# Three of four chunks of the experts' second layer by parts, one high part cast on GpSimd

## The chip, the cores and the metric

The kernel runs on one core of a Trainium2 chip. The metric is the time on the device in microseconds (us) of one launch, from the first instruction to the last with what lies around them. Seven things work side by side on the core and meet only through semaphores: TensorE (PE; its weight loads are listed as PEld), VectorE (DVE), ScalarE (ACT), GpSimd (POOL), SyncE (SP), and the DMA engines.

## What is computed

Two transformer layers with residuals: an attention with inverse squared distances, a mixture of 8 experts with top-2 routing, a linear attention, and a block with top-k tokens. The change is in the second, whose part of the reference is:

```python
logits = jnp.einsum('bsd,de->bse', input_emb, Wr) + br
route_w = jax.nn.softmax(logits, axis=-1)
_, topk_idx = jax.lax.top_k(route_w, TOP_K)          # 2 of 8
mask = jax.nn.one_hot(topk_idx, E, dtype=route_w.dtype).sum(-2)
routed = route_w * mask
routed = routed / routed.sum(axis=-1, keepdims=True)
h = jax.nn.relu(jnp.einsum('bsd,edh->ebsh', input_emb, W1) + b1[:, None, None, :])
expert_out = jnp.einsum('ebsh,ehd->ebsd', h, W2) + b2[:, None, None, :]
return jnp.einsum('bse,ebsd->bsd', routed, expert_out)
```

There are 8 sequences of 512 tokens, 128 features, 8 experts with 512 hidden features each. All experts are computed for all tokens, and routing weights are zero for the others. All is float32.

## The kernel before, in words

The program has two parts: the attention, up to about 900 us of the trace, and the rest (`build_rest`), which is the part that matters here.

**The stream of chunks.** The experts' work is a stream of 256 chunks `n`: block `b = n // 32` is a sequence, `k = n % 32` a place in it, `g = n // 4` the pair of sequence and expert, `i = n % 4` the quarter of the 512 hidden features. Of each chunk TensorE makes `z` (first layer, 128 hidden features by 512 tokens, `hidden(n)`), ScalarE makes `hr = relu(z + b1)` from it, and TensorE adds its share of the second layer to `y` (`expert(n)`). At step `k` of block `b` TensorE does small things of other stages, then `expert(n)`, then `hidden(n + 6)`: z runs 6 chunks ahead. `z` and `y` have two PSUM banks each, so `hidden(n)` waits for the relu of chunk n-2.

**By parts.** A float32 matmul is one `nc.tensor.matmul` that the profile shows as two instructions. The other way, `product` (L74), splits each operand in a high part (rounded to the type float32r) and a low part (the rest), and adds three matmuls: high by high, low by high, high by low. The first layer is always by parts. The second layer is by parts for the chunks that `in_parts(n)` names: from the second block on (`n >= 32`), the odd ones, two of four. For these ScalarE evicts z twice (`hr_h` at L1011, `hr` at L1013) and GpSimd subtracts (`hr_l = hr - hr_h`, L963), in order of n. The parts of the weights, `w2s`, are made once by VectorE (`split_w2`, L1438 and L1440), at steps 24 to 31 of the first block. GpSimd does nothing else in this stage.

**The other stages.** Beside the stream run, for the next sequence f = b+1, the front chain (layernorm, router, softmax, ranks, routing weights) and, for the sequence t = b-1, the tail chain (linear attention, top-k block). Which step each piece stands at is written out by hand in a `step(b, k)` for each engine. Three places matter:

- VectorE at steps 22 to 26: `hand_over` splits the next sequence's input (L1343 a cast, L1345 a subtraction), `softmax_start` ends with L1315, for which ScalarE waits with its exponential (L977) before its relus of step 23; then the tail's division (L1378 to L1387), `softmax_end`, `expert_ranks` and `routing`, which ends with `rw` (L1338).
- TensorE at step 24, ahead of `expert(n)`: `turn_routing` (L1096) transposes `rw`, and waits for it.
- VectorE at steps 29 to 31: statistics, normalized tokens (L743), their scores (L1398, L1399); TensorE at step 29 transposes the scores (L1154), and waits for them.

TensorE's order is fixed, so what it waits for holds back all that stands behind.

Of the kernel before, what the change touches and what calls it, by code (L numbers as in the profile page):

```python
# [14 lines left out]
ALU = mybir.AluOpType  # L15
# [740 lines left out]
def build_rest(nc, ctx, a, ident, front, x1, rwd, out, first):  # L756
# [10 lines left out]
    with ExitStack() as own:  # L767
        def sb(name, shape, dt=F32):
            return own.enter_context(nc.sbuf_tensor(name, shape, dt))

        def psum(name, shape):
            return own.enter_context(nc.psum_tensor(name, shape, F32))


        w1 = sb("w1", [P, NE, FF])
        w2 = sb("w2", [P, NE * NF, D])
# [45 lines left out]

        scr = w1[:, :, :].rearrange("p (i c) t -> p i c t", i=2)
        above = sb("above", [P, 2, NC])
        keep = sb("keep", [P, 2, NC])

        w2s = [sb("w2_h", [P, NE * NF // 2, D], F32R), sb("w2_l", [P, NE * NF // 2, D], F32R)]
        hrs = [sb("hr_h", [P, HR // 2, T], F32R), sb("hr_l", [P, HR // 2, T], F32R)]
        eps_dec = sb("eps_dec", [P, NC])
# [6 lines left out]

        names = """w2s lo chain_l eps_dec in_x in_b2 in_rest_x in_last_x in_front in_tail ones2 w1s chain_f chain_t
                 stats_f mv_f std_f rstd_f xn_f turn_f xT_f logits exp rw rwT_ps rwT rwd rb xs z hr y ye ya yT_ps
# [19 lines left out]
        N_F = 13  # L858
        N_T, N_R = 11, 4

# [15 lines left out]
        def score_row(t):  # L876
            return z[:, 0, :] if t == LATE else tb[:, 1, :]
# [14 lines left out]
        def in_parts(n):  # L892
            return n >= NU and n % 2 == 1

# [57 lines left out]
        @block.gpsimd  # L952
        def _(pool):
            normalize = att_gpsimd(pool)
            normalize(NQ - 3)
            normalize(NQ - 2)
            normalize(NQ - 1)
            pool.wait_ge(att["x1_out"], 16 * B)
            nc.gpsimd.memset(kv[:, :, 2 * D:2 * D + 1], 1.0).then_inc(S["ones2"], 1)
            for n in range(NU + 1, B * NU, 2):  # L960
                m = n // 2
                pool.wait_ge(S["hr"], n + 1)
                nc.gpsimd.tensor_tensor(hrs[1][:, m % (HR // 2), :], hr[:, n % HR, :],  # L963
                                        hrs[0][:, m % (HR // 2), :].bitcast(F32), ALU.subtract).then_inc(S["lo"], 1)

        @block.scalar
        def _(act):
# [38 lines left out]
            def hidden(n):  # L1006
                act.wait_ge(S["z"], n + 1)
                if in_parts(n):
                    if n == NU + 1:
                        act.wait_ge(att["x1_out"], 16 * B)  # L1010
                    nc.scalar.activation(hrs[0][:, n // 2 % (HR // 2), :], z[:, n % 2, :], ACT.Relu,  # L1011
                                         bias=b1[:, n % NU:n % NU + 1])
                nc.scalar.activation(hr[:, n % HR, :], z[:, n % 2, :], ACT.Relu, bias=b1[:, n % NU:n % NU + 1]).then_inc(S["hr"], 1)  # L1013
# [59 lines left out]
        def _(pe):  # L1073
# [101 lines left out]
            def expert(n):  # L1175
# [5 lines left out]
                if n == NF:  # L1181
                    pe.wait_ge(S["rwT"], 1)
                if n == NU + 1:
                    pe.wait_ge(S["w2s"], NE * NF)
                pe.wait_ge(S["hr"], n + 1)
                if in_parts(n):
                    pe.wait_ge(S["lo"], (n - NU) // 2 + 1)
                    m = product(nc, y[:, g % 2, :], [w[:, k // 2, :] for w in w2s],
                                [v[:, n // 2 % (HR // 2), :] for v in hrs], start=False, stop=(i == NF - 1))
                else:  # L1190
                    m = nc.tensor.matmul(y[:, g % 2, :], w2[:, k, :], hr[:, n % HR, :], start=(i == 0), stop=(i == NF - 1))  # L1191
# [87 lines left out]
        def _(dve):  # L1279
# [121 lines left out]
            def token_ranks(t, c):  # L1401

                dve.wait_ge(S["score_ps"], t + 1)
                V.tensor_scalar(scr[:, 0, c, :], score_row(t), score[:, c:c + 1], None, ALU.is_gt, ALU.add, accum_out=above[:, 0, c:c + 1])
                ins = V.scalar_tensor_tensor(scr[:, 1, c, :], score_row(t), score[:, c:c + 1],
                                             ttri[:, (NC - 1 - c) * P:(2 * NC - 1 - c) * P], ALU.is_equal, ALU.mult,
                                             accum_out=above[:, 1, c:c + 1])
                if c == NC - 1:
                    lr(t, ins)

# [24 lines left out]
            def split_w2(e):  # L1435
                chunks = slice(NF // 2 * e, NF // 2 * (e + 1))
                source = w2[:, NF * e + 1:NF * (e + 1):2, :]
                V.tensor_copy(w2s[0][:, chunks, :], source).then_inc(S["w2s"], NF // 2)  # L1438
                dve.wait_ge(S["w2s"], NF * e + NF // 2)
                V.tensor_tensor(w2s[1][:, chunks, :], source, w2s[0][:, chunks, :].bitcast(F32),  # L1440
                                ALU.subtract).then_inc(S["w2s"], NF // 2)

# [18 lines left out]
            def step(b, k):  # L1461
# [77 lines left out]
                if (b, k) == (0, 21):  # L1539
                    add_output(B - 1)  # L1540
                if b == 0 and k >= 24:
                    if k == 24:
                        dve.wait_ge(att["x1_out"], 16 * B)
                    dve.wait_ge(in_w2[k - 24], 16)
                    split_w2(k - 24)

# [78 lines left out]
```

## Time and profile before

| | us |
|---|---|
| median of 3 runs | 1420.71 |
| lowest, highest | 1420.41, 1423.08 |
| the profiled execution, its own time | 1424.09 |
| its span, first to last instruction | 1422.3 |

Busy in the span: TensorE 1386.1 us (97%), ScalarE 1099.9 (77%), VectorE 1096.4 (77%), GpSimd 835.2 (59%). The experts' stream runs from about 920 to 1385 us, of which the seven blocks with chunks by parts take from 990 to 1385; behind it stands a tail of some 38 us for the last sequence.

In rows of the timeline the first number is the start from the span's start, the second the duration, both us; then engine, line, operation, output <- inputs, shapes and the number of merged instructions, and in brackets how long the engine had been idle and what ended that. L12 is line 12 of the kernel before.

### The profile page before, as it was taken

What the parts mean: (1) busy time and instruction counts of PE and PEld (TensorE: products, weight loads), DVE (VectorE), ACT (ScalarE), POOL (GpSimd) and SP (SyncE); (2) the same over time, 40 slices, a digit from 0 to 9 for tenths busy, and PEclk for the clock granted to TensorE, in tenths of its full rate; (3) what the DMA queues carried; (4) which work ended last, traced back from release to release, by engine and by line L of the source; (5) the groups of instructions that cost most, each with busy time, mean ns of one, the idle gap of its engine ahead of it and who ended that gap; (6) DMA issues with size and microseconds to landing.
All of it is one profiled execution on the core that took longest, in us unless ns stands there. A gap on an engine that the chain in (4) does not pass through costs nothing.

```text
span 1422.3 us, 18183 instructions
## 1 busy us (share of the span) xinstructions
PE 1386.1 (97%) x6496; PEld 744.1 (52%) x6496; DVE 1096.4 (77%) x1995; ACT 1099.9 (77%) x947; POOL 835.2 (59%) x655
## 2 busy tenths in 40 slices
PE   8999999999999999999999999899999999999995
PEld 5444444444444444444444444445777777777774
DVE  7887897788888887887888788635677686786757
ACT  2799889969978978979979979945676776776751
POOL 4568777778778778768867876411333333333330
PEclk9999999999999999999999999999999999999999
DMA  3000010011101101101101012343011010110100
GB/s 113 1 17 17 24 46 17 23 27 36 24 16 46 24 16 39 30 17 31 38 16 32 17 30 68 108 142 106 1 68 60 8 68 2 67 60 9 68 1 15
DMA packets 45705, 54.99 MB, mean 39 GB/s; under 512 B 13808, under 2 KB 32368, under 8 KB 44464
## 3 DMA queue, kind: packets, MB, share of 16 engines
q1 hardware_dynamic: 45616, 53.84, 12.7%
q8 instruction: 52, 0.85, 0.3%
q14 instruction: 37, 0.30, 0.1%
HBM read 48.97 MB, written 4.85 MB: 38 GB/s over the span
## 4 chain that ended last, share of the span: by engine, by line
PE 86%; DVE 8%; ACT 5%; issue 1%; DMA 0%; DVEq 0%; SPq 0%
PE sc L406 14%; PE av L419 13%; PE z L74 12%; PE pj L74 12%; PE y L1191 8%; PE sc L401 6%; PE y L74 5%; PE pj L383 4%; PE pj L451 4%; DVE w L597 3%; PE pj L429 2%; ACT w L684 1%; ACT w L688 1%; ACT w L680 1%; DVE high L565 1%
## 5 line engine op out<-in xcount | busy, mean ns | idle before, releaser
L597 DVE TENSOR_SCALAR w<-sc 128x1024 f32<-128x1024 f32 x256 | 301.2, 1217 | 69.4 <-PE sc L406 67.3
L680 ACT ACTIVATE w<-w 128x2048 f32<-128x2048 f32 x128 | 237.6, 1904 | 123.3 <-DVE w L597 123.0
L320 POOL TENSOR_TENSOR wsum<-wsum,w 128x512 f32<-128x512 f32 x248 | 317.6, 1281 | 19.4
L963 POOL TENSOR_TENSOR hr_l<-hr,hr_h 128x512 fp32r<-128x512 f32 x112 | 149.9, 1338 | 263.0 <-ACT hr L1013 263.0
L406 PE MATMUL sc<-query,key 64*128 64x512 f32 x1024 | 243.3, 594 | 0.0
L684 ACT ACTIVATE w<-w 128x2048 f32<-128x2048 f32 x128 | 240.1, 1899 | 0.4
L688 ACT ACTIVATE w<-w 128x2048 f32<-128x2048 f32 x128 | 239.8, 1897 | 0.0
L419 PE MATMUL av<-w,vt 128*64 128x512 f32 x1024 | 233.8, 598 | 2.6 <-ACT w L688 2.5
L1013 ACT ACTIVATE hr<-z,b 128x512 f32<-128x512 f32 x256 | 173.6, 685 | 67.8 <-PE z L74 67.7
L306 POOL TENSOR_TENSOR sqq<-query 128x512 f32<-128x512 f32 x63 | 65.5, 1040 | 187.1 <-DVE query L537 153.0
L317 POOL TENSOR_TENSOR wsum<-w 128x512 f32<-128x512 f32 x124 | 158.9, 1282 | 5.2 <-ACT w L688 5.2
L74 PE MATMUL z<-xs_h,w_h 128*128 128x512 f32 x256 | 158.0, 617 | 2.4 <-ACT hr L1013 2.1
L419 PEld LDWEIGHTS av<-w,vt 128*64 128x64 f32 x1024 | 67.8, 136 | 160.1 <-issue 138.8
L1191 PE MATMUL y<-hr,w 128*128 128x512 f32 x288 | 147.5, 593 | 0.0
L406 PEld LDWEIGHTS sc<-query,key 64*128 64x128 f32 x1024 | 97.7, 187 | 73.5 <-issue 62.5
L1011 ACT ACTIVATE hr_h<-z,b 128x512 fp32r<-128x512 f32 x112 | 76.7, 685 | 69.4 <-PE z L74 68.9
L326 POOL TENSOR_TENSOR hT<-hT,gT 128x1024 f32<-128x1024 f32 x32 | 76.4, 2389 | 52.4 <-DMA hT<-head_recips 52.4
L74 PE MATMUL z<-xs_l,w_h 128*128 128x512 f32 x256 | 100.9, 394 | 0.0
L604 DVE TENSOR_TENSOR gT<-av,gT 128x512 f32<-128x512 f32 x64 | 43.9, 686 | 73.8 <-PE av L419 73.8
L401 PE MATMUL sc<-qrow,krow 64*128 64x512 f32 x512 | 94.5, 446 | 6.4 <-DVE krow L586 5.6
L74 PE MATMUL z<-xs_h,w_l 128*128 128x512 f32 x256 | 100.4, 392 | 0.0
L401 PEld LDWEIGHTS sc<-qrow,krow 64*128 64x128 f32 x512 | 38.5, 185 | 105.7 <-issue 41.0
(213 smaller groups left out, 2360.5 us busy)
## 6 DMA issues: line engine op xcount, KB each, us to landing
hT<-head_recips SPq DMA_DIRECT2D x64, 256.0 KB, 4.0
rb<-routing SPq DMA_DIRECT2D x8, 2048.0 KB, 7.1
w<-in_W SPq DMA_DIRECT2D x16, 256.0 KB, 5.1
xa<-in_X SPq DMA_DIRECT2D x8, 256.0 KB, 4.5
xc<-in_X SPq DMA_DIRECT2D x8, 256.0 KB, 2.8
x<-xc SPq DMA_DIRECT2D x8, 256.0 KB, 4.0
x<-x SPq DMA_DIRECT2D x1, 1792.0 KB, 8.1
out<-prod SPq DMA_DIRECT2D x7, 256.0 KB, 2.3
```

The source lines that it names most:

```text
L74: m = nc.tensor.matmul(out, lhsT[u], rhs[v], start=start and i == 0, stop=stop and i == 2)
L317: nc.gpsimd.tensor_tensor(wsum[:, u, :], w[:, j % 2, u, 0, :], w[:, j % 2, u, 1, :], ALU.add).then_inc(s_added, 1)
L320: nc.gpsimd.tensor_tensor(wsum[:, u, :], wsum[:, u, :], w[:, j % 2, u, c, :], ALU.add).then_inc(s_added, 1)
L401: nc.tensor.matmul(sc[:, i, v, :], krow[halves[v], j % 2, g % 2, c * P:(c + 1) * P], qrow[halves[v], j % 2, :], start=True, stop=False)
L406: m = nc.tensor.matmul(sc[:, i, v, :], key[halves[v], g % 3, c * P:(c + 1) * P], query[halves[v], g % 3, :], start=False, stop=True)
L419: m = nc.tensor.matmul(av[64 * v:64 * v + 64, :], vt[:, c, (2 * g + v) * E0:(2 * g + v + 1) * E0], w[:, j % 2, 2 * r + v, c, :], start=(c ...
L597: nc.vector.tensor_scalar(w[:, s, 2 * r:2 * r + 2, c, :], sc[:, i, :, :], 0.0, None, ALU.max).then_inc(s_d2, 1)
L680: nc.scalar.activation(w[:, j % 2, u, :, :], w[:, j % 2, u, :, :], ACT.Sqrt).then_inc(s_sqrt, 1)
L684: nc.scalar.activation(w[:, j % 2, u, :, :], w[:, j % 2, u, :, :], ACT.Ln, bias=ATT_EPS).then_inc(s_ln, 1)
L688: nc.scalar.activation(w[:, j % 2, u, :, :], w[:, j % 2, u, :, :], ACT.Exp, scale=-2.0).then_inc(s_w, 1)
L1013: nc.scalar.activation(hr[:, n % HR, :], z[:, n % 2, :], ACT.Relu, bias=b1[:, n % NU:n % NU + 1]).then_inc(S["hr"], 1)
L1191: m = nc.tensor.matmul(y[:, g % 2, :], w2[:, k, :], hr[:, n % HR, :], start=(i == 0), stop=(i == NF - 1))
```

## The change

- `in_parts(n)` now holds for three of four chunks (`n % 4` of 1, 2 and 3) from the second block on. 56 chunks more go by parts.
- For the chunks with `n % 4 == 2` (`by_pool`) ScalarE makes only `hr`, as before; GpSimd makes the high part itself, by a copy of `hr` into the float32r tile, waits for its own semaphore, and then subtracts.
- The rings of high and low parts have 5 places, not 3.
- `split_w2` casts and subtracts 384 columns for an expert, not 256, and stands at steps 25 to 32. TensorE waits for the parts of one expert at a time in the second block, not for all before its first chunk by parts.
- The low parts of W2 and a new scratch `scr` take the memory of `w1`, which is free by then. The scratch has one place for each of its two kinds, so `token_ranks` waits for its own second instruction in each of the 4 calls, not in the last one alone.

```diff
-        w1 = sb("w1", [P, NE, FF])
+        with ExitStack() as until_split:
+            w1 = until_split.enter_context(nc.sbuf_tensor("w1", [P, NE, FF], F32))
+        w2_l = sb("w2_l", [P, NE * (NF - 1), D], F32R)
+        scr = sb("scr", [P, 2, T])
...
-        w2s = [sb("w2_h", [P, NE * NF // 2, D], F32R), sb("w2_l", [P, NE * NF // 2, D], F32R)]
-        hrs = [sb("hr_h", [P, HR // 2, T], F32R), sb("hr_l", [P, HR // 2, T], F32R)]
+        w2s = [sb("w2_h", [P, NE * (NF - 1), D], F32R), w2_l]
+        HP = 5
+        hrs = [sb("hr_h", [P, HP, T], F32R), sb("hr_l", [P, HP, T], F32R)]
...
         def in_parts(n):
-            return n >= NU and n % 2 == 1
+            return n >= NU and n % NF > 0
+        def by_pool(n):
+            return in_parts(n) and n % NF == 2
+        def part(n):
+            return n // NF * (NF - 1) + n % NF - 1
...
-            for n in range(NU + 1, B * NU, 2):
-                m = n // 2
-                pool.wait_ge(S["hr"], n + 1)
-                nc.gpsimd.tensor_tensor(hrs[1][:, m % (HR // 2), :], hr[:, n % HR, :],
-                                        hrs[0][:, m % (HR // 2), :].bitcast(F32), ALU.subtract).then_inc(S["lo"], 1)
+            n_hi = 0
+            for n in range(NU, B * NU):
+                if in_parts(n):
+                    high, low = hrs[0][:, part(n) % HP, :], hrs[1][:, part(n) % HP, :]
+                    pool.wait_ge(S["hr"], n + 1)
+                    if by_pool(n):
+                        n_hi += 1
+                        nc.gpsimd.tensor_copy(high, hr[:, n % HR, :]).then_inc(S["hi"], 1)
+                        pool.wait_ge(S["hi"], n_hi)
+                    nc.gpsimd.tensor_tensor(low, hr[:, n % HR, :], high.bitcast(F32), ALU.subtract).then_inc(S["lo"], 1)
...
-                if in_parts(n):
+                if in_parts(n) and not by_pool(n):
                     if n == NU + 1:
                         act.wait_ge(att["x1_out"], 16 * B)
-                    nc.scalar.activation(hrs[0][:, n // 2 % (HR // 2), :], z[:, n % 2, :], ACT.Relu,
+                    nc.scalar.activation(hrs[0][:, part(n) % HP, :], z[:, n % 2, :], ACT.Relu,
                                          bias=b1[:, n % NU:n % NU + 1])
...
                 if in_parts(n):
-                    pe.wait_ge(S["lo"], (n - NU) // 2 + 1)
+                    if b == 1 and i == 1:
+                        pe.wait_ge(S["w2s"], 2 * (NF - 1) * (k // NF + 1))
+                    pe.wait_ge(S["lo"], part(n) - part(NU + 1) + 1)
...
-                if c == NC - 1:
-                    lr(t, ins)
+                lr(t, ins)
...
-                if b == 0 and k >= 24:
-                    if k == 24:
+                if 25 <= n < 25 + NE:
+                    if n == 25:
                         dve.wait_ge(att["x1_out"], 16 * B)
-                    dve.wait_ge(in_w2[k - 24], 16)
-                    split_w2(k - 24)
+                    dve.wait_ge(in_w2[n - 25], 16)
+                    split_w2(n - 25)
```

The instructions move at two places. On TensorE, steps 22 and 23 of the fourth block and what it transposes at step 24, before (`y` is the second layer, `z` the first):

```order
L1191 MATMUL y<-hr,w 128x512
L74 MATMUL z<-xs_h,w_h 128x512
L74 MATMUL z<-xs_h,w_l 128x512
L74 MATMUL z<-xs_l,w_h 128x512
L1145 MATMUL tb<-wo,o1T 128x128 x4
L74 MATMUL y<-hr_h,w_h 128x512
```

and with the change:

```order
L74 MATMUL y<-hr_h,w_h 128x512
L74 MATMUL y<-hr_h,w_l 128x512
L74 MATMUL y<-hr_l,w_h 128x512
L74 MATMUL z<-xs_h,w_h 128x512
L74 MATMUL z<-xs_h,w_l 128x512
L74 MATMUL z<-xs_l,w_h 128x512
L1162 MATMUL tb<-wo,o1T 128x128 x4
L74 MATMUL y<-hr_h,w_h 128x512
```

The float32 matmul of chunk 22 has become three matmuls of parts; the transposition of `rw` still stands three matmuls of `y` and three of `z` behind L1145 (L1162 now). On GpSimd, where the stream by parts begins (`L326` and the memset are what stands ahead of it; `hr_h` and `hr_l` are the high and low parts), with - before and + after:

```order
 L326 TENSOR_TENSOR hT<-hT,gT 128x1024 x3
-L959 MEMSET kv 128x4
-L963 TENSOR_TENSOR hr_l<-hr,hr_h 128x512 x112
+L971 MEMSET kv 128x4
+L981 TENSOR_TENSOR hr_l<-hr,hr_h 128x512
+L979 CAST hr_h<-hr 128x512
+L981 TENSOR_TENSOR hr_l<-hr,hr_h 128x512 x3
```

The 112 subtractions become a pattern of one cast and three subtractions for each four chunks. Over the program TensorE has 2609 such rows before and 2721 now, GpSimd 421 and 533, ScalarE 686 and 686, VectorE 1388 and 1388.

## Rows read from the trace of the kernel before

**Rows 1.** 985 to 1380 us: length, busy us (count) of PE PEld DVE ACT POOL; clock; DMA.
```profile
985.00:1380.00 395.00, 395.00 (x1734) 288.58 (x1732) 279.42 (x748) 272.73 (x429) 148.58 (x111) 1.00 0.10 38
```
**Rows 2.** Timeline of TensorE: steps 21 and 22 of the fourth block.
```profile
1143.07 0.40 PE L74 MATMUL y<-hr_h,w_h 128*128 128x512 f32 x1
...
1144.45 1.02 PE L1191 MATMUL y<-hr,w 128*128 128x512 f32 x2
...
1146.01 1.05 PE L1145 MATMUL tb<-wo,o1T 128*128 128x128 f32 x8
```
**Rows 3.** Costliest groups of GpSimd: count | busy us, mean ns of one | idle before.
```profile
L963 POOL TENSOR_TENSOR hr_l<-hr,hr_h 128x512 fp32r<-128x512 f32 x112 | 149.9, 1338 | 263.0 <-ACT hr L1013 263.0
L306 POOL TENSOR_TENSOR sqq<-query 128x512 f32<-128x512 f32 x63 | 65.5, 1040 | 187.1 <-DVE query L537 153.0 <-PE pj L451 23.1 <-PE pj L74 11.0
L292 POOL MEMSET head<- 128x64 f32 x1 | 0.2, 152 | 0.0
```
**Rows 4.** Timeline of VectorE, steps 22 to 26 of the fourth block.
```profile
1133.86 0.68 DVE L1459 TENSOR_TENSOR yT<-yT,ye 128x512 f32<-128x512 f32 x1
1134.46 1.51 DVE L1343 CAST xs_h<-xT_f 128x512 fp32r<-128x512 f32 x1
...
1137.05 0.20 DVE L1315 TENSOR_TENSOR lg<-lg,m 128x32 f32<-128x32 f32 x1
1138.39 0.22 DVE L1378 TENSOR_TENSOR den<-tb,eps_dec 128x64 f32<-128x64 f32 x1 [1.15 <-PE tb L1132]
...
1142.72 1.47 DVE L1329 TENSOR_TENSOR eq<-eq,etri 128x256 f32<-128x256 f32 x1
...
1146.40 0.91 DVE L1338 TENSOR_TENSOR rw<-rw,i 128x32 f32<-128x32 f32 x1
```
**Rows 5.** Timeline of GpSimd in the same stretch.
```profile
1133.97 1.72 POOL L963 TENSOR_TENSOR hr_l<-hr,hr_h 128x512 fp32r<-128x512 f32 x1 [2.08 <-ACT hr L1013]
...
1142.62 1.29 POOL L963 TENSOR_TENSOR hr_l<-hr,hr_h 128x512 fp32r<-128x512 f32 x1 [2.59 <-ACT hr L1013]
1145.99 1.27 POOL L963 TENSOR_TENSOR hr_l<-hr,hr_h 128x512 fp32r<-128x512 f32 x1 [2.08 <-ACT hr L1013]
```
**Rows 6.** Timeline of VectorE in the first block, where GpSimd does nothing.
```profile
967.62 0.42 DVE L1343 CAST xs_h<-xT_f 128x512 fp32r<-128x512 f32 x1
...
972.58 0.43 DVE L1329 TENSOR_TENSOR eq<-eq,etri 128x256 f32<-128x256 f32 x1
```
**Rows 7.** Timeline of TensorE: the transpositions of `rw` and of the scores.
```profile
1148.29 0.60 PE L1096 MATMUL fa<-ident,rw 128*8 128x128 f32 x4
...
1156.66 0.60 PE L1154 MATMUL tb<-ident,score 128*128 128x128 f32 x4
```
**Rows 8.** Timeline of ScalarE: relu of chunk 22, exponential, relu of chunk 23.
```profile
1135.07 0.69 ACT L1013 ACTIVATE hr<-z,b 128x512 f32<-128x512 f32 x1 [1.18 <-PE z L74]
...
1137.28 0.23 ACT L977 ACTIVATE pr<-lg 128x32 f32<-128x32 f32 x1 [0.23 <-DVE lg L1315]
...
1137.99 0.68 ACT L1013 ACTIVATE hr<-z,b 128x512 f32<-128x512 f32 x1
```
**Rows 9.** Timeline of VectorE: normalized tokens, scores.
```profile
1152.92 1.11 DVE L743 TENSOR_SCALAR xn_t<-x,mv_t,rstd_t 128x128 f32<-128x128 f32 x4
1154.07 1.67 DVE L1398 TENSOR_TENSOR prod<-xn_t,wrt 128x512 f32<-128x512 f32 x1
1155.78 0.69 DVE L1399 TENSOR_REDUCE score<-prod 128x4 f32<-128x512 f32 x1
```
**Rows 10.** Groups of VectorE by shape: one expert's subtraction in `split_w2`.
```profile
L1440 DVE TENSOR_TENSOR w_l<-w,w_h 128x256 fp32r<-128x256 f32 x8 | 3.4, 426 | 0.8
```
**Rows 11.** Timeline of VectorE: the next group after the splits; the end of the last ranks.
```profile
983.37 0.75 DVE L1452 SCALAR_TENSOR_TENSOR ye<-y,b,rb 128x512 f32<-128x512 f32 x1 [1.52 <-PE y L1191]
...
1416.64 0.08 DVE L1405 DVE_READ_ACCUMULATOR w<-tb,score,ttri 128x1 f32 x1
1416.76 0.16 DVE L1412 TENSOR_TENSOR above<-above 128x4 f32<-128x4 f32 x1
```

More of the change, by code:

```diff
@@ L821, in build_rest @@
         score = sb("score", [P, NC])
-        scr = w1[:, :, :].rearrange("p (i c) t -> p i c t", i=2)
         above = sb("above", [P, 2, NC])
         keep = sb("keep", [P, 2, NC])
-        w2s = [sb("w2_h", [P, NE * NF // 2, D], F32R), sb("w2_l", [P, NE * NF // 2, D], F32R)]
-        hrs = [sb("hr_h", [P, HR // 2, T], F32R), sb("hr_l", [P, HR // 2, T], F32R)]
+        w2s = [sb("w2_h", [P, NE * (NF - 1), D], F32R), w2_l]
+        HP = 5
+        hrs = [sb("hr_h", [P, HP, T], F32R), sb("hr_l", [P, HP, T], F32R)]
         eps_dec = sb("eps_dec", [P, NC])
@@ L835, in build_rest @@
         fa = psum("fa", [P, T])
-        names = """w2s lo chain_l eps_dec in_x in_b2 in_rest_x in_last_x in_front in_tail ones2 w1s chain_f chain_t
+        names = """w2s lo hi chain_l eps_dec in_x in_b2 in_rest_x in_last_x in_front in_tail ones2 w1s chain_f chain_t
                  stats_f mv_f std_f rstd_f xn_f turn_f xT_f logits exp rw rwT_ps rwT rwd rb xs z hr y ye ya yT_ps
@@ L858, in build_rest @@
         N_F = 13
-        N_T, N_R = 11, 4
+        N_T, N_R = 14, 7
         LATE = B - 2
@@ L1182, in expert @@
                     pe.wait_ge(S["rwT"], 1)
-                if n == NU + 1:
-                    pe.wait_ge(S["w2s"], NE * NF)
                 pe.wait_ge(S["hr"], n + 1)
                 if in_parts(n):
-                    pe.wait_ge(S["lo"], (n - NU) // 2 + 1)
-                    m = product(nc, y[:, g % 2, :], [w[:, k // 2, :] for w in w2s],
-                                [v[:, n // 2 % (HR // 2), :] for v in hrs], start=False, stop=(i == NF - 1))
+                    if b == 1 and i == 1:
+                        pe.wait_ge(S["w2s"], 2 * (NF - 1) * (k // NF + 1))
+                    pe.wait_ge(S["lo"], part(n) - part(NU + 1) + 1)
+                    m = product(nc, y[:, g % 2, :], [w[:, part(k), :] for w in w2s],
+                                [v[:, part(n) % HP, :] for v in hrs], start=False, stop=(i == NF - 1))
                 else:
@@ L1403, in token_ranks @@
                 dve.wait_ge(S["score_ps"], t + 1)
-                V.tensor_scalar(scr[:, 0, c, :], score_row(t), score[:, c:c + 1], None, ALU.is_gt, ALU.add, accum_out=above[:, 0, c:c + 1])
-                ins = V.scalar_tensor_tensor(scr[:, 1, c, :], score_row(t), score[:, c:c + 1],
+                V.tensor_scalar(scr[:, 0, :], score_row(t), score[:, c:c + 1], None, ALU.is_gt, ALU.add, accum_out=above[:, 0, c:c + 1])
+                ins = V.scalar_tensor_tensor(scr[:, 1, :], score_row(t), score[:, c:c + 1],
                                              ttri[:, (NC - 1 - c) * P:(2 * NC - 1 - c) * P], ALU.is_equal, ALU.mult,
                                              accum_out=above[:, 1, c:c + 1])
-                if c == NC - 1:
-                    lr(t, ins)
+                lr(t, ins)
             def kept(t):
@@ L1435, in split_w2 @@
             def split_w2(e):
[L1436 to L1441, printed above, removed]
+                parts = slice((NF - 1) * e, (NF - 1) * (e + 1))
+                source = w2[:, NF * e + 1:NF * (e + 1), :]
+                V.tensor_copy(w2s[0][:, parts, :], source).then_inc(S["w2s"], NF - 1)
+                dve.wait_ge(S["w2s"], (NF - 1) * (2 * e + 1))
+                V.tensor_tensor(w2s[1][:, parts, :], source, w2s[0][:, parts, :].bitcast(F32),
+                                ALU.subtract).then_inc(S["w2s"], NF - 1)
             def weigh(g):
```

## The prediction

> **What bounds the kernel now.** I read the page first (TensorE busy 97% of the span), then the busy time of the stretch with chunks by parts [rows 1]: TensorE is busy in all 395.00 of 395 us at clock 1.00, VectorE in 279.42, ScalarE in 272.73, GpSimd in 148.58. The list of waits names no stall of TensorE there. So before the change TensorE's own instructions set the time of this stage, and whatever others wait for is slack. The second thing to read is therefore how much slack the others have: the timeline of one block, engine by engine. I take the fourth block; the blocks two to seven have the same pattern.
>
> **What TensorE gains.** A step with the second layer by parts, first layer included, lasts 1144.45 - 1143.07 = 1.38 us; one with a float32 matmul 1146.01 - 1144.45 = 1.56 [rows 2]. The change turns 56 of the latter (8 groups in 7 blocks) into the former: 56 x 0.18 = 10.1 us less, if nobody keeps TensorE waiting. The three matmuls ask for a low part (semaphore `lo`), which the single one did not.
>
> **What GpSimd gets.** For four chunks it had 2 subtractions of 1.34 us mean [rows 3], 2.7 us; now 3 and a cast. No cast by GpSimd is in the trace. Bounds: a memset of 64 columns took 0.15 us, which neither reads nor covers 512; a subtraction, with two inputs, 1.34. Between them lies a square of 512 columns, whose two inputs are the same tile, at 1.04 [rows 3]. I take 1.04, the row nearest in size and kind. That makes 3 x 1.34 + 1.04 = 5.1 us against 1.56 + 3 x 1.38 = 5.7 us of TensorE for four chunks even where nothing else stands between them; and z runs six chunks ahead. So GpSimd is nearly full but does not become the bound by itself. The Trainium skill (GPSIMD Engine Reference, Performance versus the Vector engine) has 769 ns for a tight loop with one input over 512 elements; with it the estimate at the end would be some 3 us lower. No run here shows it.
>
> **What this does to VectorE.** This is the term that decides. Rows 4 and 5 side by side: GpSimd's subtraction is issued at 1133.97, while VectorE runs a two-input addition (1133.86 to 1134.54), and takes 1.72 us instead of 1.29, until 1135.69. VectorE's cast, issued at 1134.46, ends at 1135.97 and took 1.51 us; in the first block, where GpSimd is idle, it took 0.42 [rows 6]. L1329 took 1.47 beside the subtraction of 1142.62, and 0.43 without [rows 4 to 6]; L1338 took 0.91 beside that of 1145.99. So an operation of VectorE with two SBUF inputs, or such a cast, and one of GpSimd exclude each other for their whole length, and GpSimd's pending one came ahead of VectorE's next (1133.97 against 1134.46). The Trainium skill (SBUF — State Buffer, Who interferes with whom) says the same of the exclusion, and adds that it is the order of issue that decides; it does not say who goes first when both wait, and its rule would leave more to VectorE than I count. Operations that read PSUM I leave out.
>
> Now the chain from VectorE's cast to `rw`, which TensorE transposes at step 24. Before, `rw` is done at 1146.40 + 0.91 = 1147.31 and TensorE comes for it at 1148.29 [rows 4, 7]: 0.98 us of slack, of which two steps made shorter (18 and 22) take 0.36. Left: 0.6. In this stretch VectorE has only one pause, 1.15 us before L1378 [rows 4]. The change puts four more GpSimd operations here, cast and subtraction of chunks 22 and 26, while before there were four subtractions (21, 23, 25, 27). Worked with the durations above:
> - The relu of chunk 22 ends at 1135.76 [rows 8]. The cast of 22 waits for VectorE's own, runs 1135.97 to 1137.0; VectorE's L1345 goes behind it, to 1137.6; GpSimd's subtraction of 22 to 1138.8; L1315 behind that, at 1138.8 instead of 1137.25. Of these 1.6 us the pause takes 1.15, so VectorE is 0.4 us late.
> - ScalarE waits for L1315 before its exponential and then makes the relus of chunk 23: 1140.3 instead of 1138.67 [rows 8]. TensorE's z of chunk 25 needs it at about 1140.2: a stall of 0.1.
> - The subtraction of 23 moves from the pause onto L1321 (+0.7 or so), that of 25 onto L1327 (+0.7), the cast of 26 onto L1328 (+0.9), the subtraction of 26 onto L1329 (where 25 was before), that of 27 onto L1330 (+1.1; it was on L1338 with 0.7). `rw` is then done at 1150.3, or at 1150.9 if the subtraction of 29 meets L1338 too. TensorE is there at 1148.0.
> So it waits 2.3 to 2.9 us; with a cast of 0.65 us the same count gives 1.8. I take 2.5. This happens in the six blocks that prepare a next sequence.
>
> The scores have less slack still: done at 1155.78 + 0.69 = 1156.47, fetched at 1156.66 [rows 7, 9]. TensorE comes 0.18 earlier (step 26). The new pair of chunk 30 ends its subtraction about 0.7 us into the four normalizations of L743, and the one of 31, which now delays L1398 (1.67 us, [rows 9]), can get between them. Bounds: 0 if ScalarE's square root, which leads this chain, comes as early against TensorE as before and VectorE wins each meeting; 2.1 if 30, 31 and 33 all meet something. I take 0.9, six times. In the last block, without front chain, 0.5 in all.
>
> **Edits with small or no cost.** `split_w2`: 0.43 us for 256 columns [rows 10], so some 0.2 us more per expert for cast and subtraction of 384, 1.6 us in all on VectorE; behind the splits VectorE pauses 1.52 us before its next group [rows 11], and no GpSimd work or TensorE wait is near. Without that cover it would be 1.6. ScalarE's count does not change. The extra waits in `token_ranks`: a linked instruction starts 0.12 us after the place where an unlinked one does (1416.64 to 1416.76, [rows 11]); six of them stand in the tail, 0.7 us; the others lie beside TensorE's work. The new memory places cost nothing: `w1` is long read.
>
> **The sum**, against the profiled execution's 1424.09: -10.1 + 6 x (2.5 + 0.9) + 0.5 + 0.7 = +11.5 us, 1435.6. That execution lay 3.4 us above the median, so against the median: 1420.71 + 11.5 = 1432.2.
>
> **Rivals.**
> - *The gain arrives* (the other side: faster). Mechanism: at steps 18 to 24 VectorE is let in between GpSimd's operations, or the two interleave finer than I count, so that `rw` and the scores are later by less than their slack. Then -10.1 + 0.7 = -9.4, 1411.3; with half a microsecond left per block, 1414. It decides for faster as long as the two waits together stay under (10.1 - 0.7) / 6 = 1.6 us per block. For it: TensorE has no wait at all now, VectorE a quarter of its time free [rows 1]. Against: the chain to `rw` has hardly any of this free time, and 1.75 us of it are already such waits (1.47 - 0.43, and 0.91 - 0.20, the length of L1315, which has the same size) [rows 4, 6].
> - *VectorE goes first when both wait.* Then GpSimd gets in only behind operations that do not exclude it (L1320, L1452, L1334, L1337): four waits of about 1.1 us in place of 1.75, 1.0 us of stall after the slack, and 0.6 at the scores. -10.1 + 0.7 + 6 x 1.6 = about 0: 1421. Against it: the order at 1133.97 [rows 4, 5].
> - *Every meeting is a full one*: 2.9 and 2.1 per block: -10.1 + 1.2 + 6 x 5.0 = +21.1, 1442. A cast slower than a subtraction adds to it. Also here would be a case in which the low parts themselves come late, TensorE waiting at `y`; against it stand the six chunks of lead, over 7 us.
> - That the change doesn't do what it says I give nothing: the order of instructions shows 112 more on TensorE and on GpSimd.
>
> **How the numbers follow.** Forecast (stalls of 2.4 to 4.8 us per block together, 1425 to 1441): 0.60. Gain arrives (1410 to 1417): 0.24. VectorE first (1417 to 1424): 0.10. Every meeting full, above 1441: 0.06. A measurement of this kernel tells 0.2%, 2.8 us, from no change. Faster by more: 0.26; within: 0.09; slower by more: 0.65. The range goes from 1411, the low case nearly whole, to 1441.
>
> **What would show it.** In the profile after: TensorE no longer 395 of 395 busy between the blocks, with waits at the transposition of `rw` on L1338's successor and at that of the scores; L1345, L1315, L1321, L1328 and L1330 of VectorE a microsecond longer than now; GpSimd at some 5 us of 7 busy; its cast near 1.04. I would be wrong if TensorE shows no wait there, or if `rw` is ready before 1148.0 on the present scale.

## The result, and the profile with the change

| | before | with the change |
|---|---|---|
| median, us | 1420.86 (5 runs) | 1447.26 (5 runs) |
| lowest, highest | 1420.41, 1423.08 | 1445.55, 1447.87 |
| profiled execution, its span | 1424.09, 1422.3 | 1445.73, 1443.9 |

The ratio is 1.0173, 95% interval 1.0162 to 1.0185: 26.4 us slower. The direction was the forecast one, the time lies 15 us above the forecast 1432.2 and 6 above the range. The change lost more than twice what the sum had.

Busy times from the page, and then the window that answers to [rows 1], now 425 us long:

```profile
PE 1384.1 (96%) x6552; PEld 756.7 (52%) x6552; DVE 1132.5 (78%) x1995; ACT 1100.5 (76%) x947; POOL 949.0 (66%) x767
```

```profile
985.00:1410.00 425.00, 401.42 (x1838) 308.10 (x1837) 322.26 (x765) 276.13 (x431) 260.41 (x222) 0.98 0.09 34
```

TensorE was busy in 395 of 395 us; now it idles in 23.6 of 425, and its mean granted clock is 0.98. No other engine is full: VectorE is at 76% there, GpSimd at 61%. What TensorE and ScalarE wait for in this stretch (us in total, times, longest):

```profile
PE z L74 <- ACT hr L1030: 12.3, 6, 2.1
PE fa L1113 <- DVE rw L1355: 9.4, 6, 1.6
ACT std_t L749 <- DVE mv_t L734: 12.1, 6, 2.0
ACT pr L994 <- DVE lg L1332: 6.9, 6, 1.1
```

The second row is the predicted wait. The first, the larger one, the prediction names only for another chunk (0.1 us at chunk 25) and never at this place: from the third block on, z of chunk 13 waits at TensorE's step 7 for the relu of chunk 11. ScalarE's relu stands behind its square root L749, and that waits for VectorE's statistics (third row).

**The predicted wait** (timeline of TensorE, fourth block, step 23 and the transposition; it answers to [rows 7]):

```profile
1152.38 0.40 PE L74 MATMUL z<-xs_l,w_h 128*128 128x512 f32 x1
1154.36 0.60 PE L1113 MATMUL fa<-ident,rw 128*8 128x128 f32 x4 [1.58 <-DVE rw L1355]
```

From start to start 1.98 us where back to back it is 0.23: 1.75 us lost. VectorE and GpSimd ahead of it, answering to [rows 4] and [rows 5]:

```profile
1139.22 1.51 DVE L1360 CAST xs_h<-xT_f 128x512 fp32r<-128x512 f32 x1
1140.76 0.98 DVE L1362 TENSOR_TENSOR xs_l<-xT_f,xs_h 128x512 fp32r<-128x512 f32 x1
...
1142.10 0.83 DVE L1332 TENSOR_TENSOR lg<-lg,m 128x32 f32<-128x32 f32 x1
...
1144.61 1.65 DVE L1404 TENSOR_TENSOR x<-x,bo 128x512 f32<-128x512 f32 x1
...
1149.52 1.40 DVE L1346 TENSOR_TENSOR eq<-eq,etri 128x256 f32<-128x256 f32 x1
1150.95 1.40 DVE L1347 TENSOR_TENSOR gt<-gt,eq 128x256 f32<-128x256 f32 x1
```

```profile
1138.72 1.72 POOL L981 TENSOR_TENSOR hr_l<-hr,hr_h 128x512 fp32r<-128x512 f32 x1 [1.90 <-ACT hr L1030]
1140.57 0.62 POOL L979 CAST hr_h<-hr 128x512 fp32r<-128x512 f32 x1
1141.28 1.60 POOL L981 TENSOR_TENSOR hr_l<-hr,hr_h 128x512 fp32r<-128x512 f32 x1
...
1148.56 0.65 POOL L979 CAST hr_h<-hr 128x512 fp32r<-128x512 f32 x1
1149.29 2.79 POOL L981 TENSOR_TENSOR hr_l<-hr,hr_h 128x512 fp32r<-128x512 f32 x2
```

The mechanism is as told: L1362, L1332, L1346 and L1347 (successors of L1345, L1315, L1329 and L1330) each last until a GpSimd operation has ended, and up to their own length more. L1332, 0.20 us before, ends at 1142.93, where the subtraction beside it ends at 1142.88; L1347, 0.42 us before (L1330), ends at 1152.35, 0.27 us behind the two subtractions, which end at 1152.08. GpSimd's cast takes 0.62 and 0.65 us here, not 1.04 (median of the 56 casts 0.622, longest 1.087).

**The wait that was not foreseen** (ScalarE and TensorE, fourth block, steps 7 and 8):

```profile
1118.50 0.21 ACT L749 ACTIVATE std_t<-mv_t 128x4 f32<-128x4 f32 x1 [2.03 <-DVE mv_t L734]
```

Before the change it was the other way round. VectorE had its statistics (`mv_t`) ready at 1113.75, ScalarE's root came at 1115.01, and VectorE waited for the root. So the chain had 1.26 us of slack at this place (timeline of VectorE, kernel before, same block):

```profile
1113.47 0.28 DVE L734 BATCH_NORM_AGGREGATE mv_t<-stats_t 128x2 f32<-128x6 f32 x3
...
1115.25 0.18 DVE L740 RECIPROCAL rstd_t<-std_t 128x4 f32<-128x4 f32 x1 [1.50 <-ACT std_t L749]
```

With the change, on TensorE again:

```profile
1117.47 0.39 PE L74 MATMUL y<-hr_l,w_h 128*128 128x512 f32 x1
...
1119.91 0.50 PE L74 MATMUL z<-xs_h,w_h 128*128 128x512 f32 x1 [2.06 <-ACT hr L1030]
...
1121.00 1.91 PE L1208 MATMUL y<-hr,w 128*128 128x512 f32 x2
```

From start to start it is 2.44 us, so 2.2 are lost. And behind it the same instructions take nearly double: a float32 matmul 1.91 us, where at step 4 it took 1.02. TensorE's clock, in windows around it (length, PE busy, granted clock, DMA):

```profile
1119.00:1120.00 1.00, 0.09 (x1) 1.00 0.00 0
1120.00:1122.00 2.00, 2.00 (x6) 0.59 0.04 8
1122.00:1124.00 2.00, 2.00 (x6) 0.56 0.00 0
1124.00:1126.00 2.00, 2.00 (x13) 1.00 0.00 0
```

After two microseconds of idling the granted clock falls from 2.4 to 1.2 GHz for part of these windows, and comes back. That happens behind five of the six such waits; behind the one at 1366, as long as the others (2.0 us), the clock stays at 1.00, and no run shows why. The six waits of 1.58 us at `rw` have no such fall behind them.

**Where the time went**, by the distance from step 0 of one block to that of the next (start of the first second-layer matmul; before 1047.54 to 1104.93, after 1044.96 to 1106.60): it was 57.39 us, and is 61.6 in each of five blocks, 21.08 us in all. The block before them lost 0.56. From the last block's step 0 to the end it is 90.98 us against 87.81, 3.17 us. That is 24.8. The profiled pair differs by 21.7 only, because step 0 of the second block came at 986.96 against 990.09 us. Of these 3.1 us 2.2 lie ahead of the stream, in work that the change doesn't touch, and 0.9 in the first block (66.56 against 67.49). Three experiments whose first block is that of the kernel before took 66.65 to 66.76 for it, so it is the trace of the kernel before that is the odd one there; in the kernels of the experiments step 0 of the second block lies anywhere between 987.2 and 989.8.

### The profile page after: what moved, and what is told of

Same layout as the page of the kernel before. It is cut to its first block, busy times and chain, and to the rows that moved or that the text cites. A ratio compares the mean times of both kernels' runs of the same rounds, so it can differ in the third digit from the quotient of the medians.

```text
span 1443.9 us, 18481 instructions
## 1 busy us (share of the span) xinstructions
PE 1384.1 (96%) x6552; PEld 756.7 (52%) x6552; DVE 1132.5 (78%) x1995; ACT 1100.5 (76%) x947; POOL 949.0 (66%) x767
## 4 chain that ended last, share of the span: by engine, by line
PE 70%; DVE 19%; ACT 6%; issue 4%; DMA 0%; DVEq 0%; SPq 0%; ACTq 0%
PE sc L406 13%; PE av L419 13%; PE pj L74 11%; PE z L74 6%; PE sc L401 6%; PE pj L383 4%; PE pj L451 4%; PE y L1208 4%; PE y L74 3%; DVE w L597 3%; PE pj L429 2%; DVE scr L1422 2%; ACT w L684 1%; ACT w L688 1%; ACT w L680 1%
## 5 line engine op out<-in xcount | busy, mean ns | idle before, releaser
L981 POOL TENSOR_TENSOR hr_l<-hr,hr_h 128x512 fp32r<-128x512 f32 x168 | 226.2, 1351 | 149.1 <-ACT hr L1030 144.0
L74 PE MATMUL z<-xs_h,w_h 128*128 128x512 f32 x256 | 139.7, 546 | 15.0 <-ACT hr L1030 14.3
L326 POOL TENSOR_TENSOR hT<-hT,gT 128x1024 f32<-128x1024 f32 x32 | 76.4, 2388 | 51.8 <-DMA hT<-head_recips 51.8
L1208 PE MATMUL y<-hr,w 128*128 128x512 f32 x176 | 94.7, 621 | 0.0
```

The lines of the kernel that those rows point to most:

```text
L74: m = nc.tensor.matmul(out, lhsT[u], rhs[v], start=start and i == 0, stop=stop and i == 2)
L981: nc.gpsimd.tensor_tensor(low, hr[:, n % HR, :], high.bitcast(F32), ALU.subtract).then_inc(S["lo"], 1)
```

## The experiments

Theory A: GpSimd's operations exclude VectorE's, VectorE comes late with `rw` and with the statistics, and TensorE waits for both. Rivals: B, the waits come from something else in the change (the links in `token_ranks`, the waits for low parts); C, ScalarE is the short one; D, the clock falls for another reason than the wait. All ratios are to the kernel before on the same chip. The differences in us to the change are between medians that come from different chips; the medians of the kernel before on these chips lie between 1420.9 and 1423.0.

### GpSimd's load alone, on the kernel before

```diff
             for n in range(NU + 1, B * NU, 2):
                 m = n // 2
+                if n % NF == 3:
+                    pool.wait_ge(S["hi"], n_hi)
+                    n_hi += 2
+                    pool.wait_ge(S["hr"], n)
+                    nc.gpsimd.tensor_copy(idle_h[:, :], fixed).then_inc(S["hi"], 1)
+                    pool.wait_ge(S["hi"], n_hi - 1)
+                    nc.gpsimd.tensor_tensor(idle_l[:, :], fixed, idle_h[:, :].bitcast(F32), ALU.subtract).then_inc(S["hi"], 1)
```

> The kernel before, whose results stay as they are, with the GpSimd work of the change alone: for each chunk with n % 4 == 2 from the second block on GpSimd waits for its relu, casts 512 columns of W2 into a tile that nobody reads, and subtracts. TensorE, ScalarE and VectorE have their old instructions, and nobody waits for the new ones. Theory A (GpSimd's operations keep VectorE from SBUF, and VectorE's lateness is what TensorE waits for): the two stalls of the changed kernel appear though TensorE has nothing new, somewhat shorter since TensorE needs 1.4 us more per block here: 10 to 25 us over the kernel before. Theory B (the stalls come from TensorE's waits for low parts, or from the links in the token ranks): no change, within 1 us.

1434.75 us, ratio 1.0085 [1.007, 1.010]: in theory A's range, but with one of its two stalls only. TensorE's only wait in the stretch of seven blocks is

```profile
PE fa L1107 <- DVE rw L1349: 8.2, 6, 1.4
```

Nothing on TensorE asks for the new operations, so B's wait for low parts is not needed for this one. Yet the wait at z is missing: extra load alone doesn't make it. It uses up the slack, though. In the fourth block the statistics are ready at 1117.11 and the root starts at 1117.15, 0.04 us later where it was 1.26, and step 7 is 0.1 us longer than before. In the last block TensorE also waits 1.3 us for `xn_t`, which it did not before.

### The same places, but memsets

```diff
+                if n % NF == 3:
+                    pool.wait_ge(S["hr"], n)
+                    for i in range(2):
+                        pool.wait_ge(S["hi"], n_hi)
+                        n_hi += 1
+                        nc.gpsimd.memset(idle[:, :], 0.0).then_inc(S["hi"], 1)
```

> The kernel before with two memsets of 1024 columns by GpSimd, into a tile that nobody reads, at the places where the run with the extra load had its cast and its subtraction; all results as before. They read nothing from SBUF. Theory A (a GpSimd operation stops VectorE through its reads from SBUF, two inputs or a cast, not by being there): no stall at the transposition of rw, 1421 to 1424 us. Rival (any GpSimd operation in SBUF stops VectorE for its length): the stall of 1.54 us comes back in six blocks, 1430 to 1436.

1424.0 us, ratio 1.0007 [0.9998, 1.0016]: no change that can be told, as theory A has it, and a block takes 57.40 us. The memsets lie right over VectorE's operations:

```profile
1133.00 2.06 POOL L969 MEMSET idle<- 128x1024 f32 x2
```

```profile
1133.19 0.69 DVE L1353 TENSOR_TENSOR xs_l<-xT_f,xs_h 128x512 fp32r<-128x512 f32 x1
...
1134.24 0.20 DVE L1323 TENSOR_TENSOR lg<-lg,m 128x32 f32<-128x32 f32 x1
```

The same two took 0.98 and 0.83 us beside casts and subtractions. So it is GpSimd's reads from SBUF that stop VectorE's operations with two SBUF inputs, not its presence. The Trainium skill (SBUF — State Buffer, Who interferes with whom) says so too: a VectorE instruction with two SBUF inputs contends with a GpSimd instruction that reads SBUF, not with one that only writes it. The trace agrees, 0.69 against 0.98 us.

For another kind of VectorE operation the rival is right. In the last block TensorE waits 0.63 us for `xn_t`, for which it did not wait before, and the four normalizations (one SBUF tensor in, with two scalars per partition) take 2.58 us instead of 1.11:

```profile
1376.47 1.97 POOL L969 MEMSET idle<- 128x1024 f32 x2
```

```profile
1377.20 2.58 DVE L743 TENSOR_SCALAR xn_t<-x,mv_t,rstd_t 128x128 f32<-128x128 f32 x4
```

The last of the four also meets a subtraction, which starts at 1378.41. In the fourth block a pair of memsets alone stretches them: the first two of the four begin under the second memset and take 0.61 and 0.41 us, the other two 0.33. A memset does hold up these one-input operations.

### The links alone, on the kernel before

```diff
-                if c == NC - 1:
-                    lr(t, ins)
+                lr(t, ins)
```

> The kernel before with one piece of the change: each of the four token_ranks calls waits for its second instruction. Theory A (GpSimd's share): VectorE gets 0.4 to 0.5 us later per block in a stretch with slack; only the tail sees it: +0.5 to +1.5 us. Theory B (the links make the statistics of step 9 late and so cause the stall of z at step 7): TensorE idles at z in six blocks, +6 us or more.

1422.77 us, ratio 1.0002 [0.9993, 1.0012]. The interval holds no change and all of theory A's range; rival B's 6 us are out. In the trace the blocks take 57.35 to 57.39 us, as before: the statistics come 0.35 us later and still 0.91 us ahead of the root. From the last block's step 0 to the end it is 88.54 us against 87.81, so the links cost 0.7 us in the tail and nothing in the blocks.

### The change without the links

The four calls get eight separate scratch places (the two of `scr`, a new one, and `x_first`, `qT`, `o1T` and the two halves of `kv`, which are idle then), so only the fourth is linked.

```diff
-                V.tensor_scalar(scr[:, 0, :], score_row(t), ...
+                V.tensor_scalar(a, row, ...
...
-                lr(t, ins)
+                if c == NC - 1 or t == LATE:
+                    lr(t, ins)
```

> The changed kernel with eight scratch places for the token ranks (three of 2 KB at the scratch, and tiles that are idle at steps 2 to 5), so that only the fourth call is linked, as before the change (the sequence of the tail keeps its links). Theory A (the way to the statistics of step 9 has no slack, so each of three links at 0.12 us counts, and what they push into a GpSimd operation): z's stall of 2.2 us gets 0.4 to 1.3 us shorter in six blocks, and with a shorter pause the lowered clock may go: 1430 to 1444 us. Theory B (only GpSimd's share counts): 1446 to 1448.

1430.86 us, ratio 1.0062 [1.0047, 1.0077]: 16 us less than with the change, at the low end of theory A's range. Waits:

```profile
PE fa L1116 <- DVE rw L1358: 9.5, 6, 1.6
PE z L74 <- ACT hr L1033: 4.0, 6, 0.8
```

VectorE with the change and without links, from the ranks to the sum for the statistics (the first three rows of each are two instructions of one call and the next call's first):

```profile
1102.45 0.74 DVE L1421 TENSOR_SCALAR_CACHE_REDUCE scr<-tb,score 128x512 f32<-128x512 f32 x1
...
1103.12 0.74 DVE L1422 SCALAR_TENSOR_TENSOR scr<-tb,score,ttri 128x512 f32<-128x512 f32 x1
...
1103.90 0.75 DVE L1421 TENSOR_SCALAR_CACHE_REDUCE scr<-tb,score 128x512 f32<-128x512 f32 x1
...
1109.76 0.61 DVE L1429 TENSOR_SCALAR keep<-above 128x4 f32<-128x4 f32 x1
...
1110.47 3.20 DVE L1435 SCALAR_TENSOR_TENSOR prod<-xn_t,keep,x 128x128 f32<-128x128 f32 x4
1113.71 2.17 DVE L1442 SCALAR_TENSOR_TENSOR prod<-o,keep,prod 128x128 f32<-128x128 f32 x4
...
1117.18 0.29 DVE L730 BATCH_NORM_STATS2 stats_t<-x 128x6 f32<-128x128 f32 x1
```

```profile
1100.14 0.74 DVE L1429 TENSOR_SCALAR_CACHE_REDUCE scr<-tb,score 128x512 f32<-128x512 f32 x1
...
1100.81 0.74 DVE L1430 SCALAR_TENSOR_TENSOR scr<-tb,score,ttri 128x512 f32<-128x512 f32 x1
...
1101.48 0.74 DVE L1429 TENSOR_SCALAR_CACHE_REDUCE scr<-tb,score 128x512 f32<-128x512 f32 x1
...
1107.08 0.17 DVE L1438 TENSOR_SCALAR keep<-above 128x4 f32<-128x4 f32 x1
...
1107.35 3.63 DVE L1444 SCALAR_TENSOR_TENSOR prod<-xn_t,keep,x 128x128 f32<-128x128 f32 x4
1111.02 1.14 DVE L1451 SCALAR_TENSOR_TENSOR prod<-o,keep,prod 128x128 f32<-128x128 f32 x4
...
1113.46 0.29 DVE L730 BATCH_NORM_STATS2 stats_t<-x 128x6 f32<-128x128 f32 x1
```

A link costs 0.11 us (0.78 from 1103.12 to the next call, 0.67 without). From the first rank to the statistics it is 14.73 us with links, 13.32 without. Of these 1.41 us the three links are 0.34. The rest they push into GpSimd's operations: `keep` now meets a cast (0.61 for 0.17) and the eight 128-column operations meet more (5.37 against 4.77 us). VectorE has no pause in either. TensorE's loss at z goes from 2.2 to 0.8 us, by the same 1.4, and the clock does not fall any more: a block takes 58.57 us, 3.0 less.

### The high part on ScalarE

```diff
         def by_pool(n):
-            return in_parts(n) and n % NF == 2
+            return False
```

> The changed kernel with the high part of chunk n % 4 == 2 made by ScalarE from z, as for the others: GpSimd has 56 casts fewer (0.65 us each), ScalarE 56 evictions more (0.6 us each). Theory A (time of GpSimd under which VectorE stands): each of the two chains has two casts in it, so each stall gets shorter by 0.6 to 1.3 us and the lowered clock behind z's may go too: 1425 to 1440 us. Theory C (ScalarE is the short one: its relus are late because it is full): the stall at z grows, 1447 to 1460. If only the 56 subtractions matter: within 3 us of 1447.

1432.79 us, ratio 1.0074 [1.0059, 1.0089], 14.5 us less than with the change and in theory A's range. TensorE's waits are 6.9 us at `rw` (longest 1.2) and 7.9 us, 13 times, at z (longest 0.6): z now waits at two places in a block, neither long, and the clock stays at 1.00. The wait at `rw` got shorter by 0.4 us, less than the 0.6 to 1.3 expected, the one at step 7 by 1.4.

### TensorE kept busy in the wait

```diff
                     expert(n)
+                    if b >= 2 and k == 7:
+                        fill(nc, ta[:, :], ident, 8)
                     if n + AHEAD < B * NU:
```

> The changed kernel with eight 128x128 matmuls of the identity into the free bank ta, between expert(7) and hidden(13) of blocks three to eight, where TensorE now waits some 2.2 us for the relu. They take 1.8 us, inside the wait. Theory A (the lowered clock is a consequence of this pause): TensorE stays at full clock behind it, the stall itself stays: 6 to 10 us under the changed kernel, 1437 to 1441. Theory D (the clock falls whether or not TensorE is kept busy there): no change, 1446 to 1449.

1437.94 us, ratio 1.0113 [1.0098, 1.0128], 9.3 us under the change. Useless work in the pause makes the kernel faster. The z of 1118.53 still waits for the relu, and nothing behind it is slow (TensorE's timeline of the same step):

```profile
1116.32 1.95 PE L81 MATMUL ta<-ident 128*128 128x128 f32 x16
1118.53 0.50 PE L74 MATMUL z<-xs_h,w_h 128*128 128x512 f32 x1 [0.27 <-ACT hr L1030]
...
1119.33 1.02 PE L1208 MATMUL y<-hr,w 128*128 128x512 f32 x2
```

A block takes 59.97 us instead of 61.61. So the lowered clock costs 1.6 us in each of five blocks, about 8 us, and it is a consequence of the pause; theory D is out.

### Each place in the order moved

`stats_first`: VectorE's `result_kept` goes from step 7 behind the sum and the statistics of step 9.

```diff
                         result_others(u)
-                        result_kept(u)
+                        if t == B:
+                            result_kept(u)
...
                         tail_stats(t, 0)
+                    if k == 9 and 0 <= u < LATE:
+                        result_kept(u)
```

> The changed kernel with VectorE's result_kept (four operations of 128 columns) moved from step 7 behind the sum and the statistics of step 9, for which ScalarE's root waits; the load of GpSimd and of VectorE is unchanged. Theory A (ScalarE waits in its root and with it the relu that TensorE's z needs): the statistics come 2 us earlier, z's stall and the lowered clock behind it go, the stall at the transposition of rw stays: 1424 to 1430 us. Theory C (ScalarE is late by its own load): z waits as before, 1445 to 1449.

1428.85 us, ratio 1.0044 [1.0031, 1.0058]: 18.4 us less, with the load of every engine unchanged. What TensorE still waits for is `rw` (9.4 us, as before) and once `xn_t` (1.5). C is out for this wait.

`bias_later`: `add_bias` goes from step 23 to step 28, behind `routing`.

```diff
                         divide(t)
+                    if k == 28:
                         add_bias(t)
```

> The changed kernel with VectorE's add_bias (x + bo, 1.65 us there) moved from step 23, ahead of the expert ranks, to step 28, behind the routing. Theory A: rw comes 1.2 to 1.7 us earlier, the stall of 1.75 us at its transposition shrinks to 0 to 0.5: 1437 to 1441 us. Rival: what TensorE wins there it gives back at z, which waits for VectorE's statistics 15 steps on: the stall of 2.2 us grows by as much, and the time stays at 1445 to 1448.

1457.01 us, ratio 1.0242 [1.0228, 1.0256]: 9.8 us **slower** than the change. Both numbers missed: theory A had 1437 to 1441, and the rival, no gain at all, was not strong enough. Waits:

```profile
PE z L74 <- ACT hr L1030: 23.2, 6, 3.9
PE fa L1113 <- DVE rw L1355: 1.9, 6, 0.3
```

The wait at `rw` does go, by 7.5 us. But the one at z grows by 10.9: TensorE comes earlier, and the 1.65 us of the addition now stand in VectorE's unbroken queue toward the statistics; and behind all six pauses of 3.9 us the clock falls: its mean over the span is 0.987, lower than in the profile of any other run.

Both moves together:

> The changed kernel with both moves, of result_kept behind the statistics and of add_bias behind the routing. Theory A (the gain of 10 us by parts is real and both stalls are places in the order, not a lack of capacity): 1411 to 1417 us, 0.3 to 0.7% under the kernel before. Rival (VectorE under GpSimd's load has no slack anywhere, the stalls only move): 1420 or more.

1421.63 us, ratio 1.000 [0.9992, 1.0009]. That is above theory A's 1411 to 1417 and in the rival's range, 1420 or more. The rival's reason holds only in part: the stalls do not just move, for 25.6 us of the loss go without any load taken away, but VectorE has not enough slack for the rest. Step by step against the kernel before, a block still loses 1.38 us: 0.49 at `rw` (step 23), 0.46 and 0.21 at z (steps 7 and 27), 0.22 at the scores (step 28). The last block with the tail is 1.4 us longer than before. Without the 1.38 a block would take 57.20 - 1.38 = 55.82 us, 1.57 less than before: the gain on TensorE is real, and paid out in waits.

### Toward a faster kernel

`moved_no_links`: both moves, no links, and the transposition of `rw` at TensorE's step 25, ScalarE's copy of it at 31.

```diff
-                    if k == 24:
+                    if k == 25:
                         turn_routing(f)
...
```

> The kernel with both moves, the eight scratch places of the run without links, and the transposition of rw one step later (TensorE step 25, ScalarE's copy at 31). Theory A (every link and every meeting on VectorE's way counts, the rest is TensorE's own): of the 1.14 us per block that TensorE still waited, 0.9 go, and 0.4 in the tail: 1413 to 1417 us. Rival (ScalarE's copy so late holds back z, or the waits are ScalarE's own): 1419 to 1423.

1419.71 us, ratio 0.9983 [0.9974, 0.9992]: faster than before, but 2.7 us above the upper end of theory A's range and in its rival's (1419 to 1423). The waits that are left are not the rival's, though. A block takes 56.93 us; z keeps 0.43 us of loss, no more than in the run before it, and the transposition of the scores, which waits for VectorE, now waits 0.45. In the last block the chain of the scores shows why (VectorE, then GpSimd):

```profile
1374.08 3.26 DVE L743 TENSOR_SCALAR xn_t<-x,mv_t,rstd_t 128x128 f32<-128x128 f32 x4
```

```profile
1373.35 1.08 POOL L982 CAST hr_h<-hr 128x512 fp32r<-128x512 f32 x1
1374.51 2.49 POOL L984 TENSOR_TENSOR hr_l<-hr,hr_h 128x512 fp32r<-128x512 f32 x2
```

Four normalizations that alone take 1.1 us take 3.26 beside the cast of chunk 30 and the subtractions of chunks 30 and 31, and TensorE waits 1.5 us for them.

`moved_no_links_act`: the same with ScalarE making all high parts.

> The same, with the high part of chunk n % 4 == 2 made by ScalarE. Theory A (VectorE under GpSimd's load is the short one): 1 to 3 us less than the run beside it. Theory C (once VectorE has its place in the order, ScalarE's 0.6 us for each eviction is dearer): 2 to 8 us more than the run beside it.

1425.19 us, ratio 1.0015 [1.0007, 1.0024], 5.5 us slower than the one beside it. Theory C holds here: with VectorE's places right, ScalarE's 0.6 us cost more than GpSimd's cast. The cast on GpSimd, as the change has it, is the better place once the order fits.

`moved_but_30`: `moved_no_links`, and chunk 30 of every block and 31 of the last stay float32.

```diff
-            return n >= NU and n % NF > 0
+            return n >= NU and n % NF > 0 and n % NU != 30 and n != B * NU - 1
...
```

> The kernel with moves and without links, in which chunk 30 of every block, and chunk 31 of the last, keep the float32 matmul: eight steps on TensorE are 0.18 us longer (+1.4 us), GpSimd loses a cast and a subtraction in front of VectorE's normalized tokens and scores. Theory A (what GpSimd holds there is what the scores and z of step 29 wait for, 0.45 + 0.23 us per block, and 1.5 us once in the last block): -0.5 x 6 - 1.5 + 1.4 = -3 us against the run moved_no_links, 1415 to 1418 us. Rival (the 0.18 us each are all that changes): 1 to 2 us slower than it, 1420 to 1422.

1416.86 us, ratio 0.9962 [0.9948, 0.9975]: 5.2 us faster than the kernel before on the same chip and 30 faster than the change. TensorE's row for the stretch:

```profile
985.00:1375.00 390.00, 389.38 (x1791) 298.86 (x1790) 314.85 (x754) 272.27 (x429) 251.67 (x209) 1.00 0.10 39
```

Eight steps were given back to the slower form, and the kernel got 2.9 us faster than with them, as theory A has it. These two medians come from different chips; the traces say the same, 426.0 against 430.3 us from the second block's step 0 to the end. TensorE's waits at the scores and, in the last block, at `xn_t` are gone.

## Why the prediction was wrong

- **TensorE's gain** (-10.1): right, a little more came. It is 1.57 us per block by `both_moved`, against 8 x 0.18 = 1.44, so 11.0 in seven blocks.
- **The exclusion between GpSimd and VectorE**: right in kind, shown by the load run (+12) and the memset run (no stall at `rw`). Two things were incomplete. The cast was taken at 1.04 us and took 0.62 to 0.65 in this chain; the Trainium skill's 769 ns (GPSIMD Engine Reference, Performance versus the Vector engine) was nearer, and also too high. And the count left out VectorE's one-input operations other than casts: four L743 took 3.26 us in `moved_no_links`, `keep` of four columns 0.61 with the change, and L743 stops for memsets too.
- **The stall at `rw`** (2.5 each): right place, six times, measured 1.75. The text had said 1.8 for a cast of 0.65, and that is what came.
- **The stall at the scores** (0.9 each): did not occur with the change. This was the case named with bound 0: ScalarE leads that chain, and VectorE still waits 1.33 us for its root there (in the fourth block). TensorE loses 0.2 at z there instead.
- **"The others lie beside TensorE's work"**: this is the step that failed, and with it the sum. It judged the links, and GpSimd's new operations, at the two places where TensorE waits for VectorE directly. VectorE has no pause from the ranks (step 2) to the statistics (step 9), ScalarE waits for these before it makes relus, and TensorE needs the relu for z. This third chain was not followed. Measured from TensorE's step 0, the statistics of the fourth block were ready 3.04 us later than before (11.86 against 8.82); the slack took 1.26 of it, and TensorE itself came 0.4 earlier by its two shorter steps. That is the 2.2 us, in six blocks 13 us. Links and load only make it together: each alone, on the kernel before, left z without a wait (the links took 0.35 us of the slack, the load all of it); without links the 2.2 are 0.8.
- **The clock**: not in the forecast. The waits are long enough that five of them are followed by half the clock: another 8 us, measured by filling them.
- **The last block and the tail** (0.5 + 0.7): measured 3.2, the gain of 8 steps (1.6) included, so 4.8 without it. In it are a loss of 2.2 at z, one of some 1.8 at `xn_t` (longest wait 1.5), and 0.7 for the links in the tail. The links were priced right: `before_links`, which has nothing else, is 0.7 us longer there too.

Per block: -1.57 + 1.75 + 2.2 + 0.2 + 1.6 = +4.2 from these terms, and +4.2 were measured; with the two ends, 24.8 us.

Of the rivals "every meeting is a full one" (1442) was nearest in time, but for no reason of its own: meetings cost what was counted, at a place not counted.

## What to carry over

Before loading an engine that excludes another, follow every stretch in which the second runs without a pause to the end of its chain, through a third engine too: here VectorE to ScalarE's square root to TensorE. A link that costs nothing on its own costs its full length, and what it pushes into a meeting, once such a stretch has no slack. And where TensorE's clock falls behind a stall, the stall costs more than its length, here 3.8 us for 2.2. Moving work within the order gave back more (25.6 us) than moving load between engines (14.5); leaving eight steps in the slower form ahead of a tight chain gave some 3 us more.

## What the runs showed of the hardware

- A GpSimd cast or subtraction, which reads SBUF, stretched VectorE's operations of 0.17 to 0.43 us to 0.6 to 1.5; memsets of 1024 columns (2.06 us for two), laid over two with two SBUF inputs, stretched neither.
- The same memsets did stretch VectorE's `tensor_scalar` with one SBUF tensor, 128 columns: 0.61 us against 0.34.
- A pause of 2.06 us on TensorE was followed by half the clock five times in six; pauses of 3.9 us (`bias_later`) six times in six; pauses of 1.58 and 0.64 us were not followed by it. 1.95 us of matmuls with the identity in the pause kept the clock at 1.00 (windows of the filled run).
- A float32 to float32r cast of 512 columns took GpSimd 0.62 us in the median of 56 and 1.09 at most, a subtraction of the same size 1.27 to 1.30 where VectorE did not meet it.
